# A four-layer graph network on one core: second buffer in the projection, moved steps in layer 2 and at the end, and products moved to POOL

## What is computed

```python
# layers 0 and 1: 4 heads of 64 columns, slopes 0.01 and 0.2; layer 0 ends with elu
h = x @ W[head]
e = leaky_relu(h @ a1 + (h @ a2).T)
alpha = softmax(where(adj > 0, e, -inf), axis=-1)
out = alpha @ h
# layer 2: one head of 256 columns and a gated block of products, row by row
Wh = h @ W;  h_attn = softmax(...) @ Wh
h_enh = silu(ln(Wh @ fe1_w + b)) @ fe2_w + b
hs = ...                                   # from Wh @ W_bcdt, W_hz, out_w
g = sigmoid(silu(ln(concat([h_attn, hs]) @ g1_w + b)) @ g2_w + b)
out = ln(g * h_attn + (1 - g) * hs + h_enh)
# layer 3: scores of columns alone
h = tanh(input @ W + b);  e = h @ a;  out = softmax(where(adj > 0, e, -1e30)) @ (input @ W)
# every layer
x = layernorm(x + out)
```

## Time and profile before

| | |
|---|---|
| median of 3 runs | 3059.14 us (3057.73 to 3062.9) |
| the profiled execution | 3061.66 us, of which its span is 3059.9 |
| PE busy | 2955.5 us, 97% of the span |
| PEld | 2582.1 us, 84% |
| DVE | 2140.8 us, 70% |
| ACT | 1919.1 us, 63% |
| POOL | 1174.4 us, 38% |
| layer 0: projection, attention | 0 to 66, 66 to 848 us |
| layer 1: projection, attention | 848 to 895, 895 to 1608 us |
| layer 2: projection, steps, tail | 1608 to 1656, 1656 to 2614, 2614 to 2708 us |
| layer 3 | 2708 to 3060 us |

### The profile page before, as it was taken

One profiled execution on the slowest core, in us unless ns is written; L12 is line 12 of the kernel. 1 busy time (PEld: TensorE's weight loads), 2 busy tenths in 40 slices (PEclk: granted clock), 3 DMA queues, 4 the chain that ended last, 5 costly groups with the idle time before them and its releaser, 6 DMA issues.

```text
span 3059.9 us, 65157 instructions
## 1 busy us (share of the span) xinstructions
PE 2955.5 (97%) x24628; PEld 2582.1 (84%) x24628; DVE 2140.8 (70%) x3855; ACT 1919.1 (63%) x3414; POOL 1174.4 (38%) x1559
## 2 busy tenths in 40 slices
PE   7899999999989999999999999999999999889998
PEld 6899999999979999999997877887778778655555
DVE  5998887888878888888886556665666666562245
ACT  4777898999978999999995545444445444430000
POOL 0661365642226656564121023333323333444222
PEclk9999999999999999999999999999999999989999
DMA  8567100000100000000010000000000000000001
GB/s 286 202 209 250 48 11 11 14 11 15 60 12 14 12 12 13 12 13 11 14 34 12 4 1 4 4 1 4 1 4 4 1 1 1 2 1 1 1 17 39
DMA packets 41912, 104.55 MB, mean 34 GB/s; under 512 B 9856, under 2 KB 23424, under 8 KB 33536
## 3 DMA queue, kind: packets, MB, share of 16 engines
q1 hardware_dynamic: 39616, 101.61, 10.0%
q10 hardware_dynamic: 2112, 0.52, 0.1%
HBM read 97.73 MB, written 4.39 MB: 33 GB/s over the span
## 4 chain that ended last, share of the span: by engine, by line
PE 77%; DVE 3%; ACT 2%; POOL 1%; issue 1%; POOLq 0%; DVEq 0%; ACTq 0%
PE bank L1359 17%; PE bank L1356 16%; PE bank L1414 15%; PE bank L1452 12%; PE bank L1362 10%; PE bank L1441 2%; PE bank L1289 2%; PE bank L1428 1%; PE bank L1569 0%; ACT above L964 0%; DVE rings L1784 0%; ACT rings L1099 0%; DVE rings L1787 0%; ACT values L861 0%; DVE sums L1938 0%
## 5 line engine op out<-in xcount | busy, mean ns | idle before, releaser
L1356 PE MATMUL bank<-values,rings 128*128 128x195 bf16 x8192 | 1414.5, 247 | 37.6 <-DVE rings L1787 25.2
L1359 PE MATMUL bank<-values,rings 128*128 128x195 bf16 x8192 | 1414.6, 249 | 0.0
L964 ACT ACTIVATE above<-srow,kpass 128x512 fp8e4<-128x512 f32 x2032 | 1279.7, 709 | 128.5 <-DVE rings L1787 121.8
L1356 PEld LDWEIGHTS bank<-values,rings 128*128 128x128 fp8e4 x8192 | 806.4, 98 | 47.4 <-issue 45.3
L1359 PEld LDWEIGHTS bank<-values,rings 128*128 128x128 fp8e4 x8192 | 789.1, 96 | 0.6
L1784 DVE TENSOR_TENSOR rings<-rings,above 128x512 uint32<-128x512 uint32 x512 | 400.2, 782 | 192.3 <-PE bank L1359 168.5
L1052 ACT ACTIVATE values<-srow,cmul 128x512 f32<-128x512 f32 x256 | 205.8, 814 | 428.3 <-PE bank L1452 427.3
L1787 DVE TENSOR_TENSOR rings<-rings 128x512 uint32<-128x512 uint32 x512 | 429.7, 839 | 17.3
L1452 PE MATMUL bank<-hv,values 128*128 128x257 f32 x1792 | 420.6, 380 | 0.0
L1452 PEld LDWEIGHTS bank<-hv,values 128*128 128x128 f32 x1792 | 334.9, 190 | 69.9 <-issue 25.2
L1362 PE MATMUL bank<-values,rings 128*128 128x390 bf16 x1920 | 320.3, 329 | 11.9 <-DVE values L1820 11.9
(11 more groups left out here) (223 smaller groups left out, 3479.1 us busy)
## 6 DMA issues: line engine op xcount, KB each, us to landing
arena<-in_adj_dram SPq DMA_DIRECT2D x64, 1024.0 KB, 5.0
srow<-src_dram SPq DMA_DIRECT2D x69, 256.0 KB, 3.2
x<-in_x_dram SPq DMA_DIRECT2D x4, 1024.0 KB, 11.4
out_dram<-x SPq DMA_DIRECT2D x7, 512.0 KB, 2.9
arena<-in_L_gnn_fe_w_dram SPq DMA_DIRECT2D x2, 512.0 KB, 6.7
arena<-in_L_gnn_W_hz_dram SPq DMA_DIRECT2D x1, 1024.0 KB, 7.6
arena<-in_L_gnn_g_w_dram SPq DMA_DIRECT2D x1, 1024.0 KB, 10.8
weights<-in_L_gnn_W_dram SPq DMA_DIRECT2D x3, 256.0 KB, 3.9
```

Source lines behind the costliest of these rows:

```text
L964: last = act.activation(above[:, k % 2, q, :], srow[:, par, :], ACT.Relu, scale=BIG, bias=kpass[:, p % 2, k * Q + q:k * Q + q + 1], satura ...
L1356: pe.matmul(acc[:, 0:KW], pos[:, k % 2, q, :].bitcast(FP8)[:, rows], v[:, 0:KW], start=start, stop=final, skip_group_check=True)
L1359: last = pe.matmul(acc[:, KW:2 * KW], neg[:, k % 2, q, :].bitcast(FP8)[:, rows], v[:, KW:2 * KW], start=False, stop=final, skip_group_chec ...
```

## The change

**1. Projection.** A second xT; each quad's transposes are issued between the matmuls of the quad before (behind tile 1 and tile 3), ACT's copies of them between its copies of h. PE waits for h's copies tile by tile. Two steps of layer 1 move back one quad: ACT's elu of quad 7 and DVE's first keys.

```diff
-        xT = tiles_room[:, 0:QT * F]
+        xT_rooms = (tiles_room[:, 0:QT * F], tiles_room[:, QT * F + CHUNK * 2 * C:2 * QT * F + CHUNK * 2 * C])
...
-        xT = xT.rearrange("p (t k n) -> p t k n", t=QT, k=2)
+        xT = [xt.rearrange("p (t k n) -> p t k n", t=QT, k=2) for xt in xT_rooms]
...
-            def copy_quad_xT(l, q):
-                for half in range(2):
-                    act.wait_ge(s_xtps, q * 2 + (l * 2 * QUADS + half + 2))
-                    act.activation(xT[:, 2 * half:2 * half + 2].rearrange("p t k n -> p (t k n)"), bank[half][:, :],
-                                   ACT.Copy).then_inc(s_xt, 1)
+            def copy_xT_half(l, q, half):
+                act.wait_ge(s_xtps, q * 2 + (l * 2 * QUADS + half + 2))
+                act.activation(xT[q % 2][:, 2 * half:2 * half + 2].rearrange("p t k n -> p (t k n)"), bank[half][:, :],
+                               ACT.Copy).then_inc(s_xt, 1)
...
+                    if i % 2 == 1 and q + 1 < QUADS:
+                        copy_xT_half(l, q + 1, i // 2)
...
+                    for half in range(2):
+                        copy_xT_half(l, 0, half)
...
-                        copy_quad_xT(l, q)
-                        if l == 1 and q + AHEAD + 3 < QUADS:
-                            elu_exp(q + AHEAD + 3)
+                        if l == 1 and q in (0, 2):
+                            elu_exp(AHEAD + 3 + q // 2)
...
+            def x_across(l, q, half):
+                if l == 0 and half == 0 and q % (QUADS // X_PIECES) == 0:
+                    pe.wait_ge(s_x[q // (QUADS // X_PIECES)], 16)
+                for i in (2 * half, 2 * half + 1):
+                    if l > 0:
+                        pe.wait_ge(s_xmade, q * QT + (NORMS[l] * T + i + 1))
+                    for k in range(2):
+                        last = pe.transpose(bank[half][:, (i % 2 * 2 + k) * P:(i % 2 * 2 + k + 1) * P],
+                                            x[:, q * QT + i, k * P:(k + 1) * P], ident[:, :])
+                last.then_inc(s_xtps, 1)
...
-                for half in range(2):
-                    for i in (2 * half, 2 * half + 1):
-                        if l > 0:
-                            pe.wait_ge(s_xmade, q * QT + (NORMS[l] * T + i + 1))
-                        for k in range(2):
-                            last = pe.transpose(bank[half][:, (i % 2 * 2 + k) * P:(i % 2 * 2 + k + 1) * P],
-                                                x[:, q * QT + i, k * P:(k + 1) * P], ident[:, :])
-                    last.then_inc(s_xtps, 1)
...
+                    for half in range(2):
+                        x_across(l, 0, half)
...
-                pe.wait_ge(s_h, q * QT + (l * T + 1))
+                    pe.wait_ge(s_h, l * T + 1)
...
+                    if q > 0:
+                        pe.wait_ge(s_h, (q - 1) * QT + (l * T + i + 2))
...
-                        last = pe.matmul(bank[2 + i][:, 0:width], xT[:, i, k, :], weights[:, k, 0:width],
+                        last = pe.matmul(bank[2 + i][:, 0:width], xT[q % 2][:, i, k, :], weights[:, k, 0:width],
...
+                    if i % 2 == 1 and q + 1 < QUADS:
+                        x_across(l, q + 1, i // 2)
...
-                        if l == 0 and q % (QUADS // X_PIECES) == 0:
-                            pe.wait_ge(s_x[q // (QUADS // X_PIECES)], 16)
...
-                    if l == 1 and q == AHEAD + 1:
+                    if l == 1 and q == AHEAD + 2:
```

```diff
+                values_of(0, 2, 2)
...
-                    values_of(0, 2, g)
+                    if g + 1 < NG:
+                        values_of(0, 2, g + 1)
```

```diff
+            def first_product(l, u):
+                vtmp, factor, columns, _ = first_tiles(l, u)[1]
+                pool.wait_ge(s_vrest, first_values_before(l) + 2 * u)
+                pool.tensor_copy(vtmp[:, 0, :, D:C], factor)
+                pool.tensor_tensor(vtmp[:, 0, :, 0:D], columns, factor.to_broadcast([P, CHUNK, D]), ALU.mult)\
+                    .then_inc(s_vbigpool, 1)
...
+                    first_product(l, 1)
...
+                    for u in range(2, FIRST_CHUNKS):
+                        first_product(l, u)
...
-                    act.wait_ge((s_vbig, s_vrest)[i], first_values_before(l) + 2 * u + kind + 1)
+                    if i == 1:
+                        act.wait_ge(s_vrest, first_values_before(l) + 2 * u + kind + 1)
+                    elif l < 3 and u > 0 and kind == 1:
+                        act.wait_ge(s_vbigpool, l * (FIRST_CHUNKS - 1) + u)
+                    else:
+                        act.wait_ge(s_vbig, first_products_before(l) + (2 * u if l == 3 else u + (u > 0)) + kind + 1)
...
-                for vtmp, factor, columns, _ in first_tiles(l, u):
+                for vtmp, factor, columns, _ in first_tiles(l, u)[:2 if l == 3 or u == 0 else 1]:
```

```diff
-                    load_vector(avec[:, 0, :], A["L3_gnn_a"][:, 0])
+                    sp.dma_start(avec[:, 0, :], A["L3_gnn_a"][:, 0].partition_broadcast(P)).then_inc(s_a3, 16)
...
-        loaded_weights = [16 * 4, 16 * 13, 16 * 16, 16 * 19]
+        loaded_weights = [16 * 4, 16 * 13, 16 * 16, 16 * 18]
...
+                        if slot == 0 and i % 2 == 0 and old:
+                            scale_rows(g - 1)
...
-                            if old and i % 2 == 0:
-                                scale_rows(g - 1)
...
-                gate_tanh(EG - 1)
...
+                    if r == 4:
+                        gate_tanh(EG - 1)
...
-                g2_product(EG - 1)
...
+                    if r == 4:
+                        g2_product(EG - 1)
...
+                    if r == 0:
+                        dve.wait_ge(s_a3, 16)
...
+                dve.wait_ge(s_w, loaded_weights[3])
+                dve.memset(credits[:, 11:12], 0.0).then_inc(s_wfix, 1)
...
-                dve.wait_ge(s_w, loaded_weights[3])
-                dve.memset(credits[:, 11:12], 0.0).then_inc(s_wfix, 1)
...
+                tanh_in(4)
...
-                tanh_in(4)
```

```diff
+                make_rstd(4, QUADS - 3)
...
-                make_rstd(4, QUADS - 3)
...
+                chain.enter(NG - 3, 2)
+                for k in (2, 3, 4):
+                    output_norm(QUADS - 3, k)
...
-                chain.enter(NG - 3, 2)
-                for k in (2, 3, 4, 6, 7):
+                for k in (6, 7):
...
-                for k in (2, 3, 4, 6, 7):
-                    output_norm(QUADS - 2, k)
...
+                for k in (2, 3, 4):
+                    output_norm(QUADS - 2, k)
...
+                    if it == 0:
+                        for k in (6, 7):
+                            output_norm(QUADS - 2, k)
```

More of the change, by code:

```diff
@@ L108, in values_before, with first_products_before @@
     return sum((H - 1) * NG for m in TURN if m < l)
+def first_products_before(l):
+    return (2 + FIRST_CHUNKS - 1) * sum(m < l for m in TURN)
 def first_values_before(l):
@@ L314, in gnn_kernel @@
         s_w = sem("weights_loaded")
-        s_wfix = sem("weights_fixed")
+        s_wfix, s_a3 = sem("weights_fixed"), sem("layer3_vector_loaded")
         s_fold = sem("weights_times_a")
@@ L364, in gnn_kernel @@
         s_kfirst = sem("first_keys_made")
+        s_vbigpool = sem("values_multiplied_by_pool")
         class E:
```

## The result

| | before | changed |
|---|---|---|
| median beside each other | 3060.01 us (3057.73 to 3062.9) | 3038.62 us (3038.0 to 3040.08) |
| the same in a later series | 3059.94 us | 3037.28 us |
| profiled execution, span | 3061.66, 3059.9 | 3038.00, 3036.2 |

The ratio is 0.993 with a 95% interval of 0.9913 to 0.9947; the second time it was 0.9929 (0.9916 to 0.9943). The change makes the kernel 21 to 23 us faster, and 21.5 was forecast.

What follows compares the result with a forecast made beforehand. PE, busy 97% of the span, was taken to bound the kernel, so time is won only where it idles or runs at low clock. 0 + 3.5 + 2.3 + 5.9 + 9.4 + 3.3 + 4.4 - 7.3 = 21.5, giving 3037.6 us, range 3031 to 3043.

Steps and rivals of the forecast that it cites:

- contention: First groups: POOL's products and row factors slow DVE's masks, 0.3 a product, 1.3 us lost in all.
- Projection, layers 1 and 2: Second xT removes PE's waits for ACT's copies: 3.5 us in layer 1, 2.3 in layer 2, 0 in layer 0.
- Values ahead: Layer 0's third pass: PE's 2.9 us stop for POOL's values goes, with 3.0 of half clock behind it: 5.9.
- Products: First groups of layers 0 and 1: products moved from DVE to POOL lose 7.3 us, between +0.2 and about -11.
- The load: POOL's code load before its first product makes masks late: 2.4 us lost in layer 0, 3.0 in layer 1.
- My 0.6 for the clock: First groups of layers 0 and 1: low clock behind PE's longer stops, 0.6 us lost for both.
- The rival of the lock: DVE and POOL shut each other out for whole instructions: four products at 1.3 us, not 0.3; 3041.6; chance 0.13.
- scale_rows: Layer 2: moved into ACT's idle time, it ends PE's seven waits for it, 9.4 us gained.
- Tail: Layer 2's tail: PE's 1.87 us wait for the memset goes, plus 1.4 of low clock: 3.3, between 1.9 and 5.
- End: End of kernel: norms fitted into DVE's idle times, so the last tile's own end binds: 4.4 us, 2 to 4.6.
- The rival of the hidden load: POOL fetches its code while the copy still waits; the products cost 2.0, not 7.3: 3032.3 us; chance 0.10.
- The rival on the slower side: Layer 0: values in front of quotients put POOL behind, holding DVE, then PE, in six groups: about 3095 us; chance 0.03.

Runs made afterwards that it cites:

- e5: Kernel before with the new projection alone (second xT, transposes between the matmuls): 3048.96 us, 0.9966 of before.
- e1: Changed kernel with the first groups' products given back from POOL to DVE, all else kept: 3027.10 us, 0.9892 of before.
- e3: Kernel before with only the products moved to POOL: 3070.09 us, 1.0036 of before.
- e10: The changed kernel run once more, unaltered, as a reference: 3037.28 us.
- e2: Changed kernel plus a small POOL multiplication right behind the all-reduce, so the code load starts there: 3031.85 us, 0.9908 of before.
- e6: Kernel before with only the values one group ahead in pass 1 of layer 0: 3056.81 us, 0.9990 of before.
- e7: Kernel before with only ACT's scale_rows moved one slot ahead: 3049.19 us, 0.9972 of before.
- e4: Changed kernel with POOL making only the products of chunks 2 and 3, chunk 1 back on DVE: 3030.05 us, 0.9904 of before.
- e8: Kernel before with only the steps of layer 2's tail moved, without scale_rows: 3056.51 us, 0.9992 of before.

## Why the prediction was right

The waits that the forecast named went, and the new ones came where it put them; the contention was of another kind than it took. The total came out within 1 us, and that close it is luck: by the marks the gains were 33.4 where 28.8 were forecast, and the loss was 9.6 where 7.3 was. Of the 23.8 that this leaves the medians show 21.4, because the two profiled executions lie 2.3 further apart than the medians.

- **Projection, layers 1 and 2: 3.5 + 2.3 forecast, 5.4 + 4.0 measured (5.3 + 4.0 in e5).** The mechanism was right and each term too small. It took the idle time in the row as the price of a wait. PE's rows of transposes and matmuls overlap by 0.16 to 0.17, and a wait between them also costs that overlap: 0.57 of period for 0.34 of idle time. Layer 0: 0 forecast, 0.0 in the mean of all traces, single ones within 1.5 of it.
- **Values ahead: 5.9 forecast, 5.8 in this pair of profiles, 4.4 or 3.1 against the other traces, 2.2 timed.** The stop went. How long the clock stays low behind it differs by execution, and the six us were the longest of six.
- **Products: -7.3 forecast, -9.6 by the marks, -8 to -11.5 timed.** The load was named, placed and sized right in layer 0: the product ended at 81.0 (81.0 to 81.3 forecast), and the mask came 2.2 late (2.4). In layer 1 the load took 8.03 instead of 6.8, the product only 1.04 instead of 1.3, and the mask came 4.0 late (3.0). The first stop was then 1.5 longer in layer 0, not 2.4, because PE came to it later, and 4.5 in layer 1, not 3. The mis-sized term is contention. I took 0.3 a product from L1784's row and 1.3 in all, and gave the exclusive lock to a rival. The runs show 0.85 for each wide operation that meets a product, four in all, 3.4: with 2.2 and 4.0 that makes 9.6. Of the 10.4 against e1 that leaves 0.8 open. My 0.6 for the clock may be in it: behind the first late mask layer 1 lost 1.7 more, twice 0.85 and nothing for its clock of 0.50 from 906 to 912, but layer 0 lost 2.1 more, with a clock of 0.57 from 85.4 to 89.4. No run separates that.
- **The rival of the lock** was right on the mechanism. It put 1.3 on each of four products, 4 more in all, where its own row's 1.07 gives 3 more; the runs show 0.85. The Trainium skill ("SBUF — State Buffer", "Who interferes with whom") says that a DVE operation with two inputs from this memory, beside a GpSimd one that reads it, or a copy or scalar operation in a mode that uses two ports, is held for the whole instruction of a GpSimd one that was issued first, and the other way round. The trace agrees: L1856 (two inputs) and L1740 and L1815 (scalar operations) all end as if their own work began when POOL's product of 1.5 us was over, each 0.85 late, and the product is 1.49 for 1.04 behind L1823. Whether the scalar operations run in such a mode no row says.
- **scale_rows: 9.4 forecast, 10.7 measured**, 1.53 for each 1.34: the same error as in the projection.
- **Tail: 3.3 forecast, 3.2 in this pair, 2.8 to 4.0 for the part alone.** Part of the stop came back as a wait for ACT's powers, 2.7 the longest in the waits above.
- **End: 4.4 forecast, 4.3 by the marks, 4.8 timed alone.** DVE came to tile 0's sums at 3017.36, later than their matmuls, but caught up: tile 2 and tile 3 waited for PE.
- **The rival of the hidden load** is out: in the changed kernel, e3 and e10 the idle time of 6.9 to 8.0 us stands whole behind the copy, though in the changed kernel that copy had waited 4.23 and 3.82 before it. Its 2.0 was also mis-added: 7.3 without the two load terms is 1.9, and 1.3 without the stops' clock.
- **The rival on the slower side** needed POOL to fall behind by 19 us. POOL still waited 8.01 us in front of its quotient at 487.71, so it never came near.

The row that seemed to speak against the lock did not. L1784's 0.98 at 924.58 stood beside this product of POOL, half as wide:

```profile
924.23 0.79 POOL L543 TENSOR_TENSOR vtmp_pool<-hv,emul 128x256 f32<-128x256 f32 x1
```

It ends at 925.02, and L1784 at 925.56, its own 0.69 less 0.15 behind it: the same wait, short because the product was. L1885's 1.49 fits as well: POOL's L790 ran from 1759.55 to 1761.27, and L1885 ended at 1761.56, its own 0.42 less 0.13 behind it. The forecast compared lengths of rows, and should have looked up when the other engine's operation ended.

## What to carry to other kernels

When an engine that has to load code takes over work, look where the load stands in its list: here it stood behind the copy, which ran without it, and in front of the multiplication, and it did not start before that copy was done. An idle time of "issue" that costs nothing in the trace of before was a wait of 7 to 8 us once the work that others wait for stood behind it, and e2 got most of it back with one small instruction. To price two engines beside each other, line up when the one ends with when the other does. And value a removed wait by the period from start to start, which includes the overlap that the wait broke, and by more than one execution where the low clock behind it is a part of the price.

## What was not expected of the hardware

POOL's idle time for its load of code was 6.7 to 7.2 us in 32 places of the thirteen traces (one in each of layers 0, 1 and 3) and 7.5 to 7.9 in four (layer 1 of e6 and e7, layer 3 of e4 and e8). Behind the product's copy in layer 1 it was 8.03, and 7.91 and 7.84 in e3 and e10: long in all three, but little longer than the longest elsewhere. Its cause is open, no run was made for it. A wide DVE operation that began in a POOL product of 1.5 us was 0.85 us late in every case, whether it was an operation of 0.42, of 0.70 or of 1.22 us. After the same stop of 2.9 us the granted clock was 0.50 for six us in one execution, for three in four others, and did not fall in a sixth.
